# A ninth single tile in place of one block of two in a mixture-of-experts schedule

## The reference

```python
# two time-mix layers, each: normalise, project to k, v, r,
# running average of k*v along the sequence, gate, project, add
x = _layernorm(x + _L0_attn_ref(x, ...))
# feed-forward part with 8 experts, each token goes to its best 2
gate_out = einsum('bsd,ed->bse', x, Wg)
top_v, top_i = top_k(gate_out, 2)
probs = softmax(top_v)
for e in range(8):
    w_e = sum(probs * (top_i == e))
    h1 = x @ W1[e].T            # 256 -> 512
    h2 = x @ W2[e].T            # 256 -> 512
    out += ((h1 * sigmoid(h1) * h2) @ W3[e].T) * w_e     # 512 -> 256
x = _layernorm(x + out)
```

## Time and profile before

| | |
|---|---|
| median of 3 runs | 1204.03 us (1203.22 to 1205.99) |
| the profiled execution: span from first to last instruction | 1212.0 us |
| PE busy | 1091.2 us (90%) |
| PEld busy | 957.5 us (79%) |
| DVE busy | 909.5 us (75%) |
| ACT busy | 614.8 us (51%) |
| POOL busy | 652.6 us (54%) |
| mean granted TensorE clock | 0.958 of full |

### The profile page before, as it was taken

One profiled execution on the slowest core, in us unless ns is written; L12 is line 12 of the kernel. 1 busy time (PEld: TensorE's weight loads), 2 busy tenths in 40 slices (PEclk: granted clock), 3 DMA queues, 4 the chain that ended last, 5 costly groups with the idle time before them and its releaser, 6 DMA issues. The chain is left out here.

```text
span 1212.0 us, 22064 instructions
## 1 busy us (share of the span) xinstructions
PE 1091.2 (90%) x6624; PEld 957.5 (79%) x6624; DVE 909.5 (75%) x2050; ACT 614.8 (51%) x1019; POOL 652.6 (54%) x560
## 2 busy tenths in 40 slices
PE   6999999999999998757999999999999999999900
PEld 6778887777777786646888888888888999999900
DVE  5788888888888887744776766777776778888737
ACT  3345444444444444333444555555555666666528
POOL 1011554444444544665667667666573777777534
PEclk9899999999999998859999999999999999999965
DMA  4011221111121121356566657878775888998569
GB/s 157 18 53 52 53 54 53 53 52 52 52 52 52 52 53 36 76 138 180 127 150 168 158 126 168 207 200 210 182 202 156 196 248 243 241 221 246 112 190 383
DMA packets 80243, 164.34 MB, mean 136 GB/s; under 512 B 27568, under 2 KB 44976, under 8 KB 79920
## 3 DMA queue, kind: packets, MB, share of 16 engines
q1 hardware_dynamic: 49968, 127.72, 33.4%
q0 software_dynamic: 30208, 35.81, 16.8%
HBM read 118.78 MB, written 44.70 MB: 135 GB/s over the span
## 5 line engine op out<-in xcount | busy, mean ns | idle before, releaser
L1181 POOL DMA_INDIRECT x_acc<-fy_sb,pair_out x136 | 254.2, 1869 | 133.8 <-issue 56.0
L1371 PE MATMUL fring<-fxh,fw_hi 128*128 128x256 f32 (+1 forms) x704 | 236.0, 335 | 11.7 <-issue 8.0
L1373 PE MATMUL fring<-fxh,fw_lo 128*128 128x256 f32 (+1 forms) x704 | 234.2, 333 | 0.0
L1372 PE MATMUL fring<-fxl,fw_hi 128*128 128x256 f32 (+1 forms) x704 | 233.9, 332 | 0.0
L1201 ACT ACTIVATE fw_hi<-w_raw 128x1024 fp32r<-128x1024 f32 x156 | 163.4, 1054 | 107.9 <-PE fy L1416 90.1
L1263 DVE TENSOR_TENSOR fw_lo<-w_raw,fw_hi 128x1024 fp32r<-128x1024 f32 x156 | 189.6, 1219 | 15.5 <-ACT fw_hi L1201 12.4
L98 POOL DMA_INDIRECT xg<-x_src,pair_in x136 | 147.9, 1088 | 85.2 <-issue 43.6
L546 POOL TENSOR_TENSOR rs<-ve,neg_half 128x4 f32<-128x4 f32 x48 | 55.6, 1159 | 254.6 <-DVE nm L633 254.5
L88 POOL DMA_INDIRECT slot_list<-pairs,slot_u x128 | 144.5, 1129 | 50.3 <-issue 35.6
L870 PE MATMUL ring<-xh,w_hi 128*128 128x512 f32 x384 | 160.7, 418 | 2.1 <-issue 2.0
L1414 PE MATMUL fy<-fw_hi,gh 128*128 128x256 f32 x544 | 155.8, 286 | 0.0
(11 more groups left out here) (149 smaller groups left out, 2013.1 us busy)
## 6 DMA issues: line engine op xcount, KB each, us to landing
w_raw<-w_ffn SPq DMA_DIRECT2D x156, 512.0 KB
x_in<-h SPq DMA_DIRECT2D x16, 512.0 KB
x_src<-x SPq DMA_DIRECT2D x16, 512.0 KB
x_acc<-x SPq DMA_DIRECT2D x16, 512.0 KB
acc<-x_acc SPq DMA_DIRECT2D x16, 512.0 KB, 7.1
out<-o SPq DMA_DIRECT2D x16, 512.0 KB, 6.2
xg<-x_src,pair_in POOLq DMA_INDIRECT x136
x_acc<-fy_sb,pair_out POOLq DMA_INDIRECT x136
```

Source lines behind the costliest of these rows:

```text
L1181: nc.gpsimd.indirect_dma_start(x_acc, bass.IndirectOffsetOnAxis(pair_out[j][:, q, 0:1].bitcast(U32), 0), y[j][:, q, :], None, compute_op=A ...
L1371: nc.tensor.matmul(out, hi, rows_hi, start=dc == 0, stop=False)
L1372: nc.tensor.matmul(out, hi, rows_lo, start=False, stop=False)
L1373: last = nc.tensor.matmul(out, lo, rows_hi, start=False, stop=dc == DC - 1)
```

## The change

`SINGLES` goes from 8 to 9. `PAIRS` follows by its formula from 24 to 23. The series becomes 10 big ones, 9 times (big, single), 1 big one, 23 pairs: still 52 blocks, with 80 + 9 + 46 = 135 tiles. The pairs now begin at block 29, an odd number, where they began at block 28. Two expressions keep the PSUM bank of a pair's output opposite to what it would be by the block's parity (`PAIR_TURN`), so that the first pair still uses bank 0. The loop over (big, single) grows from 5 to 6 turns (blocks 14 to 25 where it was 14 to 23), the loop over pairs shrinks from 8 to 7 turns (34 to 47 where it was 32 to 47), and eight steps between them are written out (26 to 33 where it was 24 to 31).

```diff
-SINGLES = E
+SINGLES = E + 1
 PAIRS = (TILES_MAX - BIG * Q - SINGLES + 1) // 2
 SIZES = [Q] * 10 + [Q, 1] * SINGLES + [Q] * (BIG - SINGLES - 10) + [2] * PAIRS
 BLOCKS = len(SIZES)
+PAIR_TURN = (BLOCKS - PAIRS) % 2
...
             last = (BLOCKS - 3) // 2 * 2
+            steady = (pairs_from + 5) // 2 * 2
...
-            peeled(mixed_end - 2, pairs_from + 4)
-            loop(pairs_from + 4, last)
+            peeled(mixed_end - 2, steady)
+            loop(steady, last)
             peeled(last, BLOCKS + 2)
...
-                    bank, n = (j if tiles == 2 else k), min(tiles, 2)
+                    bank, n = ((j + PAIR_TURN) % 2 if tiles == 2 else k), min(tiles, 2)
...
-                        bank = 1 - j if tiles == 2 else k
+                        bank = (1 - j + PAIR_TURN) % 2 if tiles == 2 else k
```

## The result

| | before | after |
|---|---|---|
| median | 1203.5 us (6 runs) | 1197.47 us (6 runs) |
| ratio of after to before | | 0.9939, 95% interval 0.9915 to 0.9962 |
| profiled execution, span | 1212.0 us | 1196.5 us |

The ratio stands for -7.3 us (-10.2 to -4.6), the medians are 6.0 us apart. One run of the changed kernel, 1866.65 us at a granted clock of 0.556, is left out of the ratio.

The account below looks back on a forecast made before the run. PE was taken to bound the pair stage. 4.89 us more up to the pairs and 8.93 less behind gave -4.04, or -4.40 without a soft piece; the middle, -4.2, from 1204.03 gave 1199.8 us, range 1198.3 to 1202.6.

Parts of the forecast that it names:

- PE bounds the pair stage, and the norm phase moves with it: Pair stage: PE busy 50.00 of 50 us, so what PE saves there comes off the total one for one.
- The single's cost, and the seam, by starts of blocks: From block 24 to the first pairs: 69.79 us after the change against 64.90 before, 4.89 more; a single about 4.8.
- the soft piece: Old block 26: the single's outputs took 1.86 us against 1.50 elsewhere; if tied to that place, balance -4.40, not -4.04.
- One pair period less is to run, 8.93: Pair stage, behind the first pair: one pair fewer takes 8.93 us of PE's time off the path.
- the sum: Expert phase from block 24, by starts of blocks: 4.89 us more, one pair period of 8.93 less, balance -4.04 or -4.40.
- One hiccup of 0.53 and one of 0.16 us ... I keep them: First turns of the pair loop: hiccups of 0.53 and 0.16 us, taken to stay in the new loop.
- Rival A: Loop over (big, single): the new sixth turn is slow, 1.35 us more, giving -2.85, 1201.2 us; chance 0.22.
- The rule on matmuls of 512 columns: Single's 12 hidden matmuls: about 131 ns each by the rule, estimate -5.4; the prediction kept the row's 0.234 us each.
- Rival C: Pair stage: DMA engines become the bound, weights late in each of 22 periods; at 0.4 us, 1208.6 us; chance 0.06.
- The range: Whole kernel's time: 8 in 10 between 1198.3 and 1202.6 us, with about 1.4 for the spread of a median.

## Why the prediction was wrong

The step that failed is the one that took the pairs that stay as unchanged, at 8.93 us each. They settled at 8.82 us. The timed gains were 7.3, 9.1 and 8.2 us against the 4.2 forecast, 4.6 and 7.6 us at the old addresses. The pace accounts for 1.5 to 2.2 us of the excess; what makes the rest stays open.

- *PE bounds the pair stage, and the norm phase moves with it*: right. In the changed kernel PE is full in 1000 to 1100 us as in the earlier trace rows, and the norm phase moved with the end of the expert phase. (The reading that pairs from block 34 on are 8.93 us apart is off by one: block 34 took 8.99 us.)
- *The single's cost, and the seam, by starts of blocks*: right in size, within 0.4 us: 69.43 and 69.82 us were measured for 69.79 and, without the soft piece, 69.43. Its parts offset each other, so the closer agreement is luck. The wait of 0.24 us for issue is gone in every program with nine singles, the one with 24 pairs too, and stood (0.19 to 0.25 us) in every program that has a big block behind the one that follows the last single. It belongs to that place, as the prediction suspected, but with it went 0.16 us of the block and not 0.36.
- *"One pair period less is to run, 8.93"*: right for the one, but the step took as given that the other 22 keep their 8.93 us. They went to 8.82. This is the term that failed: not in the sum at all, 21 periods at 0.10, 2.2 us. In the stretch from block 24 on, 268.8 - 267.3 = 1.5 us of it arrived, 1.2 of them behind the start of block 39, where no profile of the two programs has a wait. That the addresses decide where the pace settles is shown, in both directions and in two programs; that they make the *time* differ is not resolved by the timed runs (4.5 us in one comparison, 0.6 in the other).
- *"One hiccup of 0.53 and one of 0.16 us ... I keep them"*: wrong in kind, by the other profiles: no profile at those addresses had less idling. PE waits there for rows that are held up by the adds of blocks before: 8.5 us with three big blocks in a row, 3.5 with two (0.7, for issue, in the profile on record), 0.9 and 1.3 with a single between the last two, all at the old addresses. The last two groups differ by about 1 us in the mean, which would close 5.6 against the 4.4 of the sum. That is not shown: the 0.7 of the first group lies below both values of the second, and the kernel with 8 singles and 23 pairs, with two in a row at other addresses, waited 0.0. That three in a row cost more is one profile, of a long execution.
- *Rival A, a slow sixth turn*: did not come, and the pattern it rested on was none: two slow turns in one execution out of 16 profiled.
- *The rule on matmuls of 512 columns*: going by the row was right, for the single's 12 hidden ones took 2.80 to 2.89 us in the changed kernel too, 0.23 to 0.24 us each. The Trainium skill, page "TensorE: Matmul & The Clock Gate", section "Back-to-back issue gap", gives about 131 ns in a steady stream with weight loads. This case's traces do not agree with it: no profile has matmuls of 512 columns in the expert phase closer than 228 ns in the mean of five.
- *Rival C, DMA as the bound*: didn't come as forecast, but a relative of it did: in some executions PE waits in the first pairs for what the adds hold up. With 8 singles, the waits are 0.0 us at a pace of 8.98, 0.7 and 3.5 at 8.93, 0.0 at 8.82, 2.7 at 8.77, 3.5 and 6.4 at 8.72. If a faster PE runs into those adds sooner, the first pairs take back part of what the pace gives, and the kernel before with moved addresses is no faster for it. The rows lean that way, with one exception (0.0 at 8.82) and one to two profiles each; it is argued, not shown.
- *The range*: it used three runs that lay 2.8 us apart. Later sets of runs of the same kernel reached from 1201.7 to 1215.4 us. The first five expert blocks, equal in all programs, took 84.7 to 95.4 us, and the profile on record had the worst of them. The three runs happened to lie close together; a range of 4 us was too narrow for that scatter, apart from the failed term.

No version beat the change by more than its interval: 96 or 128 bytes more changed the pace and not the time. Eight singles and 23 pairs, 134 tiles, ran 10.0 us under before, but the worst case of the routing needs 135 tiles.

## What to carry to other kernels

Count a removed block by differences between starts in the stage where PE never idles: that came out to 0.4 us, partly by luck. But don't take the rest of the stage as fixed. A table that gets shorter moves every tensor behind it in SBUF, and here 32 or 64 bytes were worth up to 0.2 us in each settled 8.9 us block, though not always in the time of the whole; to cost such a change cleanly, keep the addresses (leave the scratch as large as it was) and try padding on its own. Take a second profile of the same kernel before you read a pattern into waits of 1 us, and see whether the profiled execution is one of the longer ones among its runs.

## What the runs showed of the hardware

The pace at which back-to-back fp32r matmuls with 256 columns settled depended on where their operands lay in SBUF, in steps of 32 bytes. The same 72 matmuls and 4 transposes took 8.98, 8.93, 8.82, 8.77 or 8.72 us, and each mean came again in every program at those addresses once the pairs had settled (8.93 in three programs, 8.82 in two, 8.77 in three, 8.72 in three; 8.98 was run once). PE was busy throughout and the granted clock 1.00. At 8.93 the matmuls are 118 ns apart; the faster paces are made of stretches at 118 and at 113 ns, and the order of the stretches has a period of three blocks at two of the addresses although the loop's body is two. Before the pairs settle, stretches at 113 ns come at the addresses of 8.93 us too (8.63 and 8.64 us for a pair), so the address is not all of it. What inside the chip does this was not found. Moving the rows alone, with the weights where they were, gave the slowest value, and 17.73 us instead of 17.32 for big blocks.
